# Mode weights turned to column order during the convolutions, and the mixing stage laid out for them

## What is computed

```python
def layer0(x):                         # x = x + layer0(_gn(x))
    coeff = softmax(relu(x.mean((2,3)) @ w_c1.T) @ w_c2.T -> [B,32,4] / 30)
    w1, w2, w3 = (einsum('boe,eoc->boc', coeff, w) for w in experts)   # 3x3, per sample
    return conv(conv(conv(x, w1), w2), w3)
def layer1(x):                         # x = x + layer1(_gn(x))
    X = dht2d(x); Xr = flip_periodic(X)            # Hartley transform: real - imag
    Xc, Xrc = X[:,:,96:160,96:160], Xr[:,:,96:160,96:160]
    total = einsum('bixy,ioxy->boxy', (Xc+Xrc)/2, weight) \
          + einsum('bixy,ioxy->boxy', (Xc-Xrc)/2, flip_periodic(weight))
    return dht2d(pad(total)) / (256*256) + bias    # weight is [32,32,64,64]
```

## Time and profile before

| | |
|---|---|
| runs | 4760.87, 4747.78, 4752.64 us; median 4752.64 |
| profiled execution | 4754.18 us, span of the trace 4752.4 us |
| busy over the span | PE 4324.2 (91%), PEld 57%, DVE 61%, ACT 69%, POOL 47% |
| DMA | 1041.9 MB, mean 219 GB/s |
| stages in the trace | convolutions 3257, forward 540, mixing 259, inverse 696 us |

### The profile page before, as it was taken

The page is one execution under the profiler, slowest core; times in us unless marked ns, Lnnn a source line. Parts: engine busy times, 40 slices in busy tenths (PEclk is TensorE's granted clock), DMA queues, the critical chain, the costliest instruction groups (busy, mean ns, idle before and its releaser), DMA issues. The chain is left out here.

```text
span 4752.4 us, 121017 instructions
## 1 busy us (share of the span) xinstructions
PE 4324.2 (91%) x40114; PEld 2695.9 (57%) x40114; DVE 2883.4 (61%) x4306; ACT 3292.8 (69%) x6385; POOL 2241.6 (47%) x2115
## 2 busy tenths in 40 slices
PE   4999999999999999999999999996677656899998
PEld 2555555454454555545555555454677656788887
DVE  4555555555555555555555555555699866565555
ACT  3888888888888888888888888884466567333333
POOL 4455454554545545455454554545799765000000
PEclk9999999999999999999999999998899978999999
DMA  4867768676686766867668676687999899899999
GB/s 136 198 153 180 171 150 198 153 180 169 151 197 152 180 168 151 197 153 180 167 153 199 155 179 163 157 198 208 301 320 323 272 205 205 336 409 411 409 404 378
DMA packets 717207, 1041.90 MB, mean 219 GB/s; under 512 B 151808, under 2 KB 599072, under 8 KB 667168
## 3 DMA queue, kind: packets, MB, share of 16 engines
q1 hardware_dynamic: 683296, 1032.09, 78.0%
q10 hardware_dynamic: 33792, 8.65, 1.0%
HBM read 746.67 MB, written 293.88 MB: 219 GB/s over the span
## 5 line engine op out<-in xcount | busy, mean ns | idle before, releaser
L350 PE MATMUL bank<-ring_B,w_now 128*64 128x512 f16 (+1 forms) x14283 | 3088.6, 377 | 58.3 <-DVE w_now L558 47.8
L350 PE MATMUL bank<-ring_A,w_now 128*64 128x512 f16 (+1 forms) x14283 | 3088.5, 377 | 0.0
L350 PEld LDWEIGHTS bank<-ring_B,w_now 128*64 128x64 f16 x14283 | 1551.6, 109 | 1484.0 <-DVE w_now L558 55.9
L350 PEld LDWEIGHTS bank<-ring_A,w_now 128*64 128x64 f16 x14283 | 1551.5, 109 | 52.5
L571 DVE SCALAR_TENSOR_TENSOR ring_A<-bank,ring_A 128x512 f16<-128x512 f32 (+1 forms) x1027 | 696.8, 678 | 1140.0 <-ACT ring_A L418 1119.9
L288 ACT COPY ring_B<-ring_A 64x516 f32<-64x516 f32 x1590 | 988.1, 621 | 503.0 <-DVE ring_A L571 434.3
L290 ACT COPY ring_B<-ring_A 64x516 f32<-64x516 f32 x1059 | 658.5, 622 | 12.3
L721 POOL TENSOR_TENSOR ring_A<-xn,ring_A 128x512 f16<-128x512 f32 x515 | 582.7, 1131 | 94.5 <-POOL xn L719 89.4
L418 ACT ACTIVATE ring_A<-bank 128x512 f16<-128x512 f32 (+1 forms) x1027 | 600.0, 584 | 35.7 <-PE bank L350 25.9
L1502 DVE SCALAR_TENSOR_TENSOR i_ot<-i_ob,i_bias_bc,i_xt 128x512 f32<-128x512 f32 x512 | 366.1, 747 | 288.0 <-DMA i_xt<-x 144.7
L1446 PE MATMUL i_ob<-i_back,i_u 128*128 128x256 f32 x2048 | 529.1, 381 | 7.9 <-DVE i_ot L1502 4.5
(11 more groups left out here) (163 smaller groups left out, 4982.0 us busy)
## 6 DMA issues: line engine op xcount, KB each, us to landing
f_xt<-x SPq DMA_DIRECT2D x128, 1024.0 KB, 6.9
i_xt<-x SPq DMA_DIRECT2D x128, 1024.0 KB, 16.0
out<-i_ot SPq DMA_DIRECT2D x128, 1024.0 KB, 14.2
st_in_A<-in_x SPq DMA_DIRECT2D x65, 1024.0 KB, 7.4
st_in_B<-in_x SPq DMA_DIRECT2D x65, 1024.0 KB, 7.9
x_in_A<-in_x SPq DMA_DIRECT2D x324, 192.0 KB, 3.9
res_A<-in_x SPq DMA_DIRECT2D x324, 192.0 KB, 5.2
res_B<-in_x SPq DMA_DIRECT2D x324, 192.0 KB, 5.1
```

Source lines behind the costliest of these rows:

```text
L350: last = nc.tensor.matmul(dst[64 * half:64 * half + 64, 0:nb * IMG], w_now[n][:, w, 64 * dx:64 * dx + 64], r[side][:, kind, s0:s0 + nb, dx ...
```

## The change

**Convolutions.** `first` gets a second use, once sample 0's statistics are done: 128 partitions of `w_rows` [32 o, 65 x] and two of `w_cols` [64 x, 32 o]. In sample s SyncE loads mode rows 4s to 4s+3 of all channels (4 DMAs, each to 32 partitions, 256 bytes a piece), VectorE copies column 0 to column 64, turns the columns to the order x, o in 4 copies of 128x512 (one after each step 5 of its inner Fori), and in 4 more (after steps 27, 28, 30 and 31) a second version with x running backwards (the periodic flip). SyncE stores both to a scratch tensor `turned` [2, 64 rows, 32 i, 64 x 32 o].

**Forward.** ScalarE makes all of hi, VectorE all `y` copies; GpSimd has no part. Modes are stored in an order in which the sample stands within the row. The weights of chunks 0 and 1 are read from `turned`, in pieces of 8 KB (16 DMAs a chunk, each to 32 partitions), straight to `m_wt`, of which there are now two.

**Mixing.** Weights are the moving operand and modes the stationary one; a result partition holds (row, half, sample) and its columns (x, o). VectorE lays out both halves of the modes, ScalarE takes all four result pieces, SyncE stores a chunk in one DMA of 8 KB pieces. The inverse's constants are loaded in the middle of this stage.

**Inverse.** It reads the mixed modes in the new order and waits for no constants. The order of the constants' ky is changed to match.

```diff
 # build_convs, SyncE
             with sp.Fori(0, S) as s:
                 nxt = sp.snap((s + 1) % S)
                 n0 = sp.snap(s * NCH)
+                sp.wait_ge(turned, s * 8 + 1)
+                for j in range(4):
+                    sp.dma_start(w_rows[j * C:(j + 1) * C, :, 0:M], mode_w[:, :, bass.ds(s * 4 + j, 1), :].rearrange("i o a x -> i o (a x)")
+                                 ).then_inc(rows_here, 16)
                 with sp.Fori(0, 3) as i:
...
                     load_stat(buf, nxt2, g - 1)
+                sp.wait_ge(turned, s * 8 + 9)
+                for i in range(2):
+                    sp.dma_start(turned_d[i, bass.ds(s * 4, 4)].rearrange("y i x -> (y i) x"), w_cols[i].rearrange("p x o -> p (x o)")
+                                 ).then_inc(turned_out, 16)
                 sp.wait_ge(x1_ready, n0 + NCH + 1)
 # VectorE
+            def turn_rising(i):
+                cols = bass.ds(i * 16, 16)
+                nc.vector.tensor_copy(w_cols[0][:, cols, :], w_rows[:, :, cols].rearrange("p o x -> p x o")).then_inc(turned, 1)
+            def turn_falling(i):
+                src = w_rows[:, :, M - 16 * i:M - 16 * (i + 1):-1]
+                nc.vector.tensor_copy(w_cols[1][:, 16 * i:16 * (i + 1), :], src.rearrange("p o x -> p x o")).then_inc(turned, 1)
...
                 step(n0, 2, ("C", 0, s, None))
+                dve.wait_ge(turned_out, s * 32 + 1)
+                dve.wait_ge(rows_here, s * 64 + 64)
+                chain(nc.vector.tensor_copy(w_rows[:, :, M], w_rows[:, :, 0]), nb)
+                dve.sem_inc(passed, 1)
                 with dve.Fori(0, 4) as i:
...
+                        if t == 5:
+                            turn_rising(i)
...
+                    if t in (27, 28, 30, 31):
+                        turn_falling((27, 28, 30, 31).index(t))
                 install(2, n0 + NCH, k2)
 # the loads of weights in forward and mixing
+def load_weights(engine, turned_d, k, part, half, wt, here):
+    p = slice((2 * part + half) * C, (2 * part + half + 1) * C)
+    for t in range(ROWS):
+        r = ROWS * k + t
+        y = (M - r if half != part else r) if r else M // 2 * half
+        engine.dma_start(wt[p, t, :], turned_d[part, y]).then_inc(here, 16)
 # build_forward, ScalarE's hi and VectorE's copies
-                nc.scalar.activation(half_of(xh[g % NX], 0), half_of(xt[g % NX], 0), ACT.Copy, scale=scale_now[even][:, 4 * g:4 * g + 1]
-                                     ).then_inc(hi_act, 1)
+                for j in range(2):
...
+                    nc.scalar.activation(part(xh[g % NX]), part(xt[g % NX]), ACT.Copy, scale=scale_now[even][:, ch:ch + 1]
+                                         ).then_inc(hi_ready, 1)
...
-                copy_y(nc.vector.tensor_copy, 0, g).then_inc(y_dve, 1)
+                made = b1[buf][:, :, 0:4 * NH].rearrange("p x (c k) -> p x c k", c=4)
+                nc.vector.tensor_copy(y_mid[:, :, 4 * g:4 * g + 4], made[:, :, :, NH - 1])
+                for wc in range(2):
+                    last = nc.vector.tensor_copy(y[buf][:, wc], made[:, wc, :, 0:M].rearrange("p c (t k) -> p t c k", t=2))
+                last.then_inc(y_ready, 1)
 # build_mix, SyncE
             for k in range(NCK):
                 if k >= 2:
+                    sp.wait_ge(ft_dve, (k - 1) * NQ)
+                load_modes(k)
+                if k >= 2:
+                    sp.wait_ge(made, (k - 1) * NQ)
+                    for part in range(2):
+                        for half in range(2):
+                            load_weights(sp, turned_d, k, part, half, wt[k % 2], w_here[k % 2])
+                    store(k - 2)
+                if k == 3:
+                    sp.dma_start(back[:], spec[:, OFF_BACK:OFF_BACK + 2 * IMG]).then_inc(consts_here, 16)
...
 # build_mix, TensorE
-                    last = nc.tensor.matmul(bank[n % 2][:, x, :], wt[:, kx, :], ft[:, kx].rearrange("p t g b -> p (t g b)"),
+                    last = nc.tensor.matmul(bank[n % 2][:, x, :].rearrange("p (t o) -> p t o", t=T),
+                                            ft[:, kx].rearrange("p t g b -> p (t g b)"), wt[k % 2][:, :, kx * C:(kx + 1) * C],
                                             start=True, stop=True)
```

More of the change, by code:

```diff
@@ L127, in build_convs @@
         first = sb("first", [P, 8, 512 * 4])
+        spare = first[:].rearrange("p a b -> p (a b)")
+        w_rows = spare[:, 0:C * (M + 1)].rearrange("p (o x) -> p o x", o=C)
+        w_cols = [spare[:, 2048 * (2 + i):2048 * (3 + i)].rearrange("p (x o) -> p x o", o=C) for i in range(2)]
         bank = [[ps(f"bank{n}{i}", [P, 512]) for i in range(2)] for n in range(3)]
@@ L151, in build_convs @@
         w_ready = [sem(f"w{n}_ready") for n in range(3)]
+        rows_here, turned, turned_out = (sem(n) for n in ("rows_here", "turned", "turned_out"))
         mean_ready, gm_ready, e_ready, stq_ps, stq_ready, gap_ready, hid_ps, hid_ready, log_ps, lg_ready, exp_ready, \
@@ L780, in spectral_constants @@
     i = np.arange(M // 2)
-    below = i - i % ROWS + ROWS - 1 - i % ROWS
-    ky = np.concatenate([i, np.where(below, M - below, M // 2)])
+    ky = np.stack([i, np.where(i, M - i, M // 2)], 1).reshape(-1)
     back_h = np.concatenate([c.T[ky], s.T[ky]], 0)[:, by_pair]
@@ L1235, in _ @@
-                        sp.dma_start(to_rows(own, T - own), rows(T * k + own, T - own)).then_inc(f_here[buf], 16)
-                if k >= 2:
-                    sp.wait_ge(re_ready, (k - 1) * NQ)
-                    sp.wait_ge(im_ready, (k - 1) * NQ)
-                    for i in range(4):
-                        load_weights(sp, w, k, i, raw[buf], w_here[buf])
+                            sp.dma_start(f_raw[k % 2][p, 0], fm_d[:, :, part * M:(part + 1) * M].rearrange("b i x -> i b x")).then_inc(f_here[k % 2], 16)
@@ L1241, in _ @@
+            store(NCK - 2)
+            store(NCK - 1)
+            sp.wait_ge(consts_here, 32)
             for i in range(2):
-                sp.wait_ge(gone[i], 32 * (NCK // 2))
+                sp.wait_ge(gone[i], 16 * (NCK // 2))
         @block.tensor
@@ L1262, in quarter, with modes @@
             return slice(n % NQ * XQ, (n % NQ + 1) * XQ)
-        def weights_here(engine, n):
-            k = n // NQ
-            if k >= 2 and n % NQ == 0:
-                engine.wait_ge(w_here[k % 2], W_DMAS[1] * (k // 2))
-        def modes(engine, multiply, g, n):
+        def modes(engine, g, n, multiply):
             k = n // NQ
@@ L1302, in _, with both @@
             dve.wait_ge(masks, 1)
+            def both(n):
+                for g in range(2):
+                    last = modes(dve, g, n, multiply)
+                last.then_inc(ft_dve, 1)
             for n in range(NQ):
-                imaginary(n)
-                modes(dve, nc.vector.tensor_scalar, 1, n).then_inc(ft_dve, 1)
+                both(n)
             for n in steps:
-                take(dve, nc.vector.tensor_copy, (0,), n, taken_dve)
                 if n + NQ in steps:
-                    imaginary(n + NQ)
-                    modes(dve, nc.vector.tensor_scalar, 1, n + NQ).then_inc(ft_dve, 1)
+                    dve.wait_ge(made, n + 1)
+                    both(n + NQ)
@@ L1328, in _ @@
-            for n in range(NQ):
-                real(n)
-            for n in steps:
-                take(act, nc.scalar.copy, (1, 2, 3), n, taken_act)
-                if n + NQ in steps:
-                    real(n + NQ)
-                if n >= NQ and n % NQ == 0:
-                    store(n // NQ - 1)
-            store(NCK - 1)
+            for n in steps:
+                take(act, nc.scalar.copy, (0, 1, 2, 3), n, taken_act)
         @block.gpsimd
@@ L1343, in _, with build_inverse @@
             last.then_inc(masks, 1)
-            pool.wait_ge(masks, 1)
-            for n in range(NQ):
-                modes(pool, nc.gpsimd.tensor_scalar, 0, n).then_inc(ft_pool, 1)
-            for n in steps:
-                if n + NQ in steps:
-                    pool.wait_ge(made, n + 1)
-                    modes(pool, nc.gpsimd.tensor_scalar, 0, n + NQ).then_inc(ft_pool, 1)
-def build_inverse(nc, t_d, x1d, bias, spec, out_d, S):
+def build_inverse(nc, t_d, x1d, back, bias_bc, out_d, S):
     f32 = mybir.dt.float32
@@ L1425, in _ @@
         def _(pe):
-            pe.wait_ge(here, 32)
             def over_ky(c, n):
```

182 lines of the change are left out of this document (59 added, 123 removed).

## The result

The changed kernel takes 4900.32 us (median of 4, 4894.16 to 4907.49) against 4750.21 us for the kernel before on the same chip: a ratio of 1.031, 95% interval 1.029 to 1.0335. The forecast was 4831 us, range 4715 to 4890. The sign was right, the time lies 10 us outside the range, and the change is +150 us where +78 was forecast.

The account below looks back on a forecast made before the run. Bounds: TensorE in convolutions; VectorE, GpSimd and DMA in forward; loads in mixing; TensorE and DMA in inverse. 4754.2 + 114 (wait) + 5 (copies) - 28 (forward) - 12 (mixing) - 1 (inverse) = 4832, median 4831 us, range 4715 to 4890.

Parts of the forecast that it names:

- The new wait and its chain: Convolutions: VectorE waits 7 us for rows after step 2, delaying lo, ScalarE's copy and TensorE; 7.6 us a sample, 114 in all.
- The stall's size: Convolutions: TensorE stalls 5.5 us a sample, rows landing by 1685.5 at 201 GB/s; 2.1 us of clock loss comes on top.
- The 8 copies: Convolutions: VectorE's turning copies, 0.5 to 0.9 us each, are covered; 5 us charged, 58 us without the cover.
- rival 3: Convolutions: the copies on VectorE break ScalarE's rhythm, 58 us more, kernel 4885 us; chance 0.10.
- The 2 us that TensorE has in hand: Convolutions: work queued for TensorE, about 2 us, read from 1681.6 to 1683.6, said to cover the rising copies.
- Forward: Forward stage: 29.7 falls to 27.7 us a sample, DMA becoming the late term; 14 samples x 2.0 = 28 us gained.
- the terms, 21 and 6.1: Forward stage's DMA time a sample: 8.4 MB at 400 GB/s, 21 us; 4096 packets at 24 ns, 6.1 us.
- Mixing: Mixing stage: loads to 32 partitions stay at 210 GB/s and end last; 247 against 259 us, 12 us gained.
- rival 2: Mixing and forward weights: large pieces lift loads to 400 GB/s, 85 and 15 us gained, kernel 4745 us; chance 0.17.
- its first rule: Mixing: the Trainium skill's section on small descriptors, by which larger pieces help; the sum would fall to 4745.
- Rivals 1 and 2: First: rows ready when asked or TensorE's lead covers the wait, 4718 us, chance 0.13; second: loads at 400 GB/s, 0.17.
- both: Convolutions and mixing: no cost from the rows' wait and loads at 400 GB/s together, kernel 4631 us; chance 0.04.

Follow-up runs that it names:

- e1: Changed kernel with VectorE's wait for the rows moved from after step 2 to before each turning copy (after step 5): 4759.14 us, ratio to before 1.0022.
- e2: As e1, with the 8 turning copies of a sample left out and all transfers kept: 4689 us, period 197.2 us a sample.
- e5: As e1, with each turning copy moved inside its step, between VectorE's two lo instructions: 4695.42 us, ratio to before 0.9888.
- e11: As e5, with every store of modes in the forward stage issued twice: forward stage 565 us against 504.
- e7: As e5, with each mixing chunk's weights loaded by 4 DMAs of 1 MB, each to all 128 partitions (wrong weights): mixing stage 182 us, forward 481.
- e9: As e5, with each mixing block of 32 channels on every fourth partition instead of 32 neighbours: 4588.27 us, ratio to before 0.9673.
- e10: As e5, with a mixing chunk's weights in 4 DMAs of 1 MB, each to 32 neighbouring partitions (wrong weights): mixing stage 238 us.
- e6: As e5, with ScalarE's queue issuing mixing's loads to partitions 64 to 127: 4675.70 us, ratio to before 0.984.
- e4: Changed kernel with the stores of turned weights issued behind the next rows' loads, and the wait for those stores moved to step 5: 4859 us.
- e8: As e4, with the next rows' loads issued right behind the last store of x1, before SyncE's loop turn, turned-weight stores behind them: 4816 us.
- e12: Changed kernel with the next rows' loads issued right behind the last store of x1, turned-weight stores still ahead in the queue: 4896 us.

## Why the prediction was right or wrong

- *The new wait and its chain*: right in kind. Position, releaser, the path over `lo` and ScalarE's copy, and 2.1 us of clock are as told. VectorE asked at 1563.33, and the small copy, `bn_stats` and the path to TensorE took 4.0 us where 3.6 was summed.
- *The stall's size*: a mis-sized term. Forecast 5.5 us, measured 8.51. Set on before's time axis (VectorE's end of step 2, 1678.35 and 1563.33, laid on each other: 115.0 us), the rows landed at 1686.9 instead of 1685.5, TensorE ran dry at 1682.4 instead of 1683.6, and the path took the 0.4 us more: 1.4 + 1.2 + 0.4 = 3.0. The landing was late by the rate: from about 1563.5, when the stores are through, the rows' pieces move at some 160 GB/s and not 201. SyncE's way round its loop (5.7 us) was not in the sum either, but here it hid behind the stores; that is why taking the stores away alone gave 2.3 us and not 5. Why TensorE ran dry earlier wasn't followed up. Removing the wait's place gave 141 us (e1) where 114 was the term.
- *The 8 copies*: the step that failed. The prediction called them covered and charged 5 us; rival 3, 58 us in place of the 5, got a chance of 0.10. They cost 62 (e1 against e2). The 2 us that TensorE has in hand were read at one place, behind the weight exchange, and taken for every step. In the inner loop every copy stood between `x1` and the next `bn_stats` and `lo`, with no idle time of VectorE before or behind it, and in e1 TensorE shows small gaps in the inner loop and more in the steps from 27. e5 is the check: the same copies in the 1.9 to 2.4 us that VectorE waits inside a step cost nothing. The price was low too (1.25 us or more for half of the rising ones), and the collision with GpSimd that lengthened them, which rows 9 showed for a longer copy, is the part that e5 doesn't separate.
- *The sum of both* is why the range failed, by 10 us: forecast and rival 3 were treated as alternatives, yet they add. 4832 + 57 (copies, 62 against 5) + 27 (the wait, 141 against 114) - 14 (the three stages that gained 55 instead of 41) is 4902, the time of the profiled execution.
- *Forward*: 29.7 to 27.70 us a sample ((3898.00 - 3565.57) / 12), as forecast; `lo` fell to 1.28 us throughout. The number owes something to luck: the terms, 21 and 6.1, make 27.1, the 0.6 on top of them has no source, and the 6.1 was too high. The gain was 32 us, since all 16 samples have it and not 14. The bound named for it is only half shown (e11).

```profile
L1083 DVE SCALAR_TENSOR_TENSOR f_xl<-f_xt,f_scale_now,f_xh 128x1024 f16<-128x1024 f32 x256 | 316.4, 1277 | 72.0 <-ACT f_xh L1135 70.0
```

- *Mixing*: right in what limits it. Loads at 208 GB/s, a chunk in 32 us (30 to 33 forecast), rival 2 refuted: pieces of 8 KB didn't help, and e7 and e9 show what does. The gain was 19 us and not 12; the other 7 weren't followed up. The 4745 that the prediction puts beside its first rule is rival 2's 400 GB/s and isn't worked out from that rule.
- *Rivals 1 and 2* didn't occur. With both of their conditions made true by hand and the copies moved (e9) the kernel takes 4588 us; "both" was put at 4631.

## What to carry to other kernels

Work put into an engine that is busy 60% of the time isn't free: on the handover between two others, 7.8 us of copies a sample cost 3.9 us, and in the engine's idle time inside a step they cost nothing. Look for that idle time in the engine's timeline, and look at what GpSimd does at that moment. Terms that are priced as rivals of each other can also both come true: ask whether they add. A wait for a transfer costs by its place: ask which instructions queue behind it, and put it just ahead of the first use. When a load is slow with the DMA engines full and large pieces, look at which partitions it writes before changing its size.

## What was not expected of the hardware

- 32 neighbouring partitions took 208 GB/s, every fourth partition 407 GB/s, with the same DMAs otherwise (e9); 1 MB in one DMA changed nothing (e10); two queues on the two halves gave 262 GB/s only (e6).
- SyncE needed 3.5 to 4.6 us from its last issue in the loop's body to its first in the next pass where the queue ran empty meanwhile (e4), 5.5 to 5.9 us beside 2.1 MB of stores (changed kernel), each time with a packet of an instruction queue in between; 0.2 us with no jump in between (e8, e12).
- A VectorE copy of 128x512 f32 took about 0.6 us, and over 0.9 and up to 1.45 in just those 48 of 64 cases in which GpSimd's add of `xn` and `ring_A` ran beside it (e1).
- A gap of TensorE of about 1.8 us (1557.6 to 1559.4 in the stretch 1550 to 1560 above) left the granted clock at 1.00; after 2.35 us before the change it was 0.57 over the next 4 us, after 8.51 us 0.50 to 0.52.
